# Causal mask added by VectorE instead of by a matmul, maximum subtracted by GpSimd, in a fused attention and mixture-of-experts kernel

## The reference, cut to what matters

```python
# x, ctx: (128, 64, 128); mask: (128, 64), all False here; 16 heads of 64
def xattn(q, k, v, Wq, Wk, Wv, Wo, bo, mask):       # q = layernorm(x), k = v = ctx
    dots = einsum('bhid,bhjd->bhij', qh, kh) * SCALE
    dots = where(mask[:, None, None, :], mask_value, dots)
    dots = where(causal[None, None, :, :], mask_value, dots)
    attn = softmax(dots, axis=-1)
    out = einsum('bhij,bhjd->bhid', attn, vh)
    return out.transpose(...).reshape(b, n, h * d) @ Wo + bo

x = x + xattn(layernorm(x), ctx, ctx, Wq, Wk, Wv, Wo, bo, mask)
x = x + moe(layernorm(x))        # router, top 2 of 8 experts, gelu, gate-weighted sum
```

## Time and profile before

| | us |
|---|---|
| median of 3 runs | 1299.99 |
| lowest and highest run | 1291.49, 1300.99 |
| profiled execution, its span from first to last instruction | 1169.6 |
| the 16 groups, within the span | about 35 to 870 |

### The profile page before, as it was taken

How to read it: one execution, slowest core, us unless ns; L and a number is a source line. 1 busy time by engine, 2 the same in 40 slices (tenths; PEclk the granted TensorE clock), 3 DMA queues, 4 the chain that set the end, 5 groups by cost and what they waited for, 6 DMA issues and landing times.

```text
span 1169.6 us, 24163 instructions
## 1 busy us (share of the span) xinstructions
PE 1052.8 (90%) x6755; PEld 718.1 (61%) x6755; DVE 786.0 (67%) x2372; ACT 706.3 (60%) x1373; POOL 496.6 (42%) x592
## 2 busy tenths in 40 slices
PE   7999999999999999999999999999955999999920
PEld 6655656565655656565665656566634888888820
DVE  4757595867768586866869586776755455545538
ACT  2676676767676676767667676767641544554410
POOL 3104344443424334442424344442253677776730
PEclk7899999999999999999999999999985999999965
DMA  6000101010010101001010101000012332223259
GB/s 187 19 19 1 38 1 36 7 29 25 11 36 0 36 0 36 11 25 36 0 36 0 36 5 32 16 20 19 1 55 83 85 91 88 87 87 88 77 171 282
DMA packets 80369, 55.93 MB, mean 48 GB/s; under 512 B 7620, under 2 KB 75606, under 8 KB 80342
## 3 DMA queue, kind: packets, MB, share of 16 engines
q1 hardware_dynamic: 70000, 37.01, 11.8%
q0 software_dynamic: 8704, 17.97, 4.4%
q10 hardware_dynamic: 1638, 0.62, 0.2%
HBM read 32.22 MB, written 23.35 MB: 48 GB/s over the span
## 4 chain that ended last, share of the span: by engine, by line
PE 67%; ACT 14%; issue 7%; DVE 6%; DMA 2%; POOL 1%; DVEq 1%; ACTq 0%; SPq 0%; POOLq 0%
PE bank L708 11%; PE bank L824 10%; PE bank L709 9%; PE bank L710 9%; ACT vf L634 7%; PE bank L958 6%; PE bank L810 6%; PE bank L961 5%; PE bank L799 4%; ACT pT L607 3%; ACT pr L612 3%; PE bank L821 3%; PE bank L938 2%; DVE xs L1337 2%; PE bank L736 1%
## 5 line engine op out<-in xcount | busy, mean ns | idle before, releaser
L634 ACT ACTIVATE vf<-bank 64x512 f32<-64x512 f32 x512 | 302.2, 590 | 91.2 <-PE bank L710 80.7
L461 POOL TENSOR_TENSOR rs<-ve,half 128x4 f32<-128x4 f32 x48 | 56.5, 1176 | 272.5 <-DVE ve L994 272.5
L620 ACT ACTIVATE kf<-bank 128x512 f32<-128x512 f32 x192 | 114.8, 598 | 94.3 <-PE bank L710 84.1
L550 POOL DMA_INDIRECT mixed<-kf,ix_i x144 | 142.7, 991 | 53.9 <-issue 50.2
L810 PE MATMUL bank<-vf,pT 128*64 128x128 f32 x2048 | 139.9, 279 | 8.3 <-ACT pT L607 6.0
L810 PEld LDWEIGHTS bank<-vf,pT 128*64 128x64 f32 x2048 | 109.7, 136 | 53.8 <-issue 33.6
L507 POOL DMA_INDIRECT slots<-zrow,slot_ix x120 | 122.5, 1021 | 42.4 <-issue 42.4
L824 PE MATMUL bank<-kf,zT 128*64 128x512 f32 x512 | 138.1, 618 | 0.0
L708 PE MATMUL bank<-cTh,Ah 128*128 128x512 f32 (+1 forms) x328 | 131.1, 400 | 5.4 <-DVE cTl L1060 5.4
L456 POOL TENSOR_TENSOR idle_p<-half 128x1 f32<-128x1 f32 x88 | 17.7, 202 | 247.9 <-DVE slot_ix L1167 224.3
L708 PE MATMUL bank<-Nh,cTh 128*128 128x512 f32 x256 | 120.6, 471 | 0.0
(11 more groups left out here) (187 smaller groups left out, 1912.5 us busy)
## 6 DMA issues: line engine op xcount, KB each, us to landing
kf<-slots SPq DMA_DIRECT2D x72, 130.0 KB
xs<-in_x_dram SPq DMA_DIRECT2D x16, 256.0 KB, 3.4
c_in<-in_ctx_dram SPq DMA_DIRECT2D x16, 256.0 KB, 3.8
kf<-mixed SPq DMA_DIRECT2D x16, 256.0 KB, 4.0
vf<-mixed SPq DMA_DIRECT2D x16, 256.0 KB, 4.1
out_dram<-xs SPq DMA_DIRECT2D x16, 256.0 KB, 3.6
mixed<-kf,ix_i POOLq DMA_INDIRECT x144
vf<-in_L_ffn_W_dram SPq DMA_DIRECT2D x2, 1024.0 KB, 9.6
```

What stands on the lines that cost most here:

```text
L550: pool.indirect_dma_start(out=mixed, out_offset=bass.IndirectOffsetOnAxis(ap=ix_i[buf][:, j:j + 1], axis=0), in_=y_sb[buf][:, j, :], in_of ...
L620: act.activation(kf[:, h, :], ring[gr.bank(name)][:, :], ACT.Copy).then_inc(act_ev, 1)
L634: act.activation(vf[par][64 * par_h:64 * par_h + 64, b, 4 * q4:4 * q4 + 4, :], ring[gr.bank(name)][64 * b:64 * b + 64, :].rearrange("p (j ...
```

## The change

- The mask matmul L821 and the bf16 identity `ident_b` (one memset and one select on POOL) go; the score matmuls start their banks themselves. PE waits for the new semaphore `masked` before it writes a score bank again, instead of for `shifted`.
- DVE's `shift_half` becomes `mask_half`: DVE adds `mask_b` to the scores on the way from PSUM to `pr` (SBUF), and takes the maximum from `pr`.
- A new function `shift` on POOL subtracts the maximum in place in `pr`, twice a pair, and releases ACT's exponential through `shifted`.
- The calls of `shift` are put between POOL's norms: pair 0 of a group after `x1_norm`, pair 1 after `z2_norm`, pairs 2 and 3 after `prep`, and `send` comes behind all four.
- Before its first group DVE waits for its own last write of `mask_b`.

```diff
@@ gpsimd
+            def shift(n, par):
+
+                for t in range(2):
+                    hs = slice(8 * t, 8 * t + 8)
+                    pool.wait_ge(sm_st, 6 * n + t + 1)
+                    pool.tensor_tensor(pr[par][:, hs, :], pr[par][:, hs, :],
+                                       mx[:, par, hs].unsqueeze(2).to_broadcast([P, 8, S]),
+                                       ALU.subtract).then_inc(shifted, 1)
...
             prep(0)
             prep(1, start.done("ZB"))
+            for i in range(GP):
+                shift(i, i % 2)
...
             with pool.Fori(2, NG - 1) as g:
                 x1_norm(g - 1)
+                shift(GP * g, 0)
                 z2_norm(g - 1)
+                shift(GP * g + 1, 1)
                 prep(g + 1, group_of(g - 1).done("ZB"))
+                shift(GP * g + 2, 0)
+                shift(GP * g + 3, 1)
                 next_tokens(g - 1)
                 send(g - 1)
@@ tensor, scores
-                    pe.wait_ge(shifted, 2 * n + hf - 1)
+                    pe.wait_ge(masked, 2 * n + hf - 1)
                 heads = s_ps[hf][:, :].rearrange("p (h s) -> p h s", s=S)
-                mrow = mask_b[:, n, :].unsqueeze(1).to_broadcast([P, 8, S])
-                pe.matmul(heads, ident_b[:, :], mrow, start=True, stop=False, skip_group_check=True)
                 for b in range(2):
                     cols = slice(i * P + 64 * b, i * P + 64 * b + 64)
                     last = pe.matmul(heads[64 * b:64 * b + 64], zT[:, cols], kf[:, 8 * hf:8 * hf + 8, cols],
-                                     start=False, stop=True, skip_group_check=True)
+                                     start=True, stop=True, skip_group_check=True)
@@ vector
-            def shift_half(n, par, t):
+            def mask_half(n, par, t):
...
                 dve.wait_ge(sc_ps, 2 * n + t + 1)
-                dve.reduce_max(mx[:, par, hs], src, AX_X).then_inc(sm_st, 1)
-                dve.wait_ge(sm_st, 6 * n + t + 1)
-                dve.tensor_tensor(pr[par][:, hs, :], src, mx[:, par, hs].unsqueeze(2).to_broadcast([P, 8, S]),
-                                  ALU.subtract).then_inc(shifted, 1)
+                dve.tensor_tensor(pr[par][:, hs, :], src, mask_b[:, n, :].unsqueeze(1).to_broadcast([P, 8, S]),
+                                  ALU.add).then_inc(masked, 1)
+                dve.wait_ge(masked, 2 * n + t + 1)
+                dve.reduce_max(mx[:, par, hs], pr[par][:, hs, :], AX_X).then_inc(sm_st, 1)
```

More of the change, by code:

```diff
@@ L122, in xattn_ffn_kernel @@
     out_t = out.rearrange("(n two) s d -> (two s) n d", two=2)
-    CONSTS = 10 + 2 * E + 3 + 7
+    CONSTS = 9 + 2 * E + 3 + 6
     TAB_NEXT, TAB_ALL = 1, 19
@@ L156, in xattn_ffn_kernel @@
         ident = sb("ident", [P, P])
-        ident_b = sb("ident_b", [P, P], BF16)
         causal = sb("causal", [P, P])
@@ L281, in xattn_ffn_kernel @@
         sm_st = sem("sm_st")
+        masked = sem("masked")
         shifted = sem("shifted")
@@ L416, in _ @@
             pool.memset(ident[:, :], 0.0).then_inc(consts, 1)
-            pool.memset(ident_b[:, :], 0.0).then_inc(consts, 1)
             pool.memset(causal[:, :], 0.0).then_inc(consts, 1)
@@ L435, in _ @@
                       allow_small_or_imprecise_dtypes=True).then_inc(consts, 1)
-            pool.wait_ge(consts, CONSTS - 7)
+            pool.wait_ge(consts, CONSTS - 6)
             pool.memset(pad_rows[:, :, D:D + 1], PAD_TOKEN).then_inc(consts, 1)
@@ L440, in _ @@
             pool.affine_select(out=ident[:, :], in_=ident[:, :], compare_op=ALU.not_equal, fill=1.0,
-                               base=0, pattern=[[-1, P]], channel_multiplier=1).then_inc(consts, 1)
-            pool.affine_select(out=ident_b[:, :], in_=ident_b[:, :], compare_op=ALU.not_equal, fill=1.0,
                                base=0, pattern=[[-1, P]], channel_multiplier=1).then_inc(consts, 1)
@@ L513, in _ @@
             prep(1, start.done("ZB"))
+            for i in range(GP):
+                shift(i, i % 2)
             x1_norm(0, first=True)
+            shift(GP, 0)
             z2_norm(0, first=True)
+            shift(GP + 1, 1)
             prep(2, group_of(0, True).done("ZB"))
+            shift(GP + 2, 0)
+            shift(GP + 3, 1)
             send(0)
@@ L524, in _ @@
             x1_norm(NG - 2)
+            shift(NP - 4, 0)
             z2_norm(NG - 2)
+            shift(NP - 3, 1)
+            shift(NP - 2, 0)
+            shift(NP - 1, 1)
             next_tokens(NG - 2)
@@ L1196, in group @@
                         dve.wait_ge(t_full, 2 * n - 2)
-                    shift_half(n, par, 0)
-                    shift_half(n, par, 1)
+                    mask_half(n, par, 0)
+                    mask_half(n, par, 1)
                     if i == 0:
@@ L1218, in _ @@
             dve.tensor_copy(next_slot[:, :], region[:, :]).then_inc(w1_ok, 1)
+            dve.wait_ge(mk_ok, 8)
             group(0, first=True)
```

## The result

| | median us | lowest to highest | runs |
|---|---|---|---|
| before, timed beside it | 1297.99 | 1291.49 to 1300.99 | 4 |
| after | 1321.72 | 1310.67 to 1326.12 | 4 |

A forecast was written before the change was run, and what follows sets the result against it. The pair phase was taken as a loop of latencies through four engines, with the exponential a station. 29 us in groups, 2 in the first group and 2 behind the last send made 33 us, so 1333 us, range 1318 to 1355.

The forecast's parts named there:

- The station on POOL: POOL's subtraction between DVE's maximum and ACT's exponential: 1.04 us each, exponential 2.64 us behind DVE's start, 1.19 us late.
- Pair 0, "no change to D1": D0 to D1, DVE's starts on pairs 0 and 1: taken as zero change, 0.7 us earlier to 0.9 later.
- Pair 1, +1.44: DVE's start on pair 1 to pair 2: 1.19 us exposed delay plus 0.25 for prep holding a DVE multiply.
- Pair 2, +0.20: DVE's start on pair 2 to pair 3: 0.52 us of delay shows, minus 0.32 for the mask matmul.
- Pair 3, +0.16: DVE's start on pair 3 to the next group's first head product: exponential at 2.64 us instead of 2.48.
- A group, +1.8: The four pairs' delays together, 1.8 us a group, 29 us for 16; the range was about 0.9 to 3 us.
- First group, 2 us: Pair 0's shift stands behind prep(1) on POOL, 2.6 us later than wanted, of which 2 us were taken.
- Behind the last send, 2 us (1 to 5): After the last group, x1_norm waits on POOL behind the later send, with no head phase to hide it: 2 us.
- With the 130.4 us around it: Time of the median outside the profiled span of 1169.6 us, added to the new span of about 1203 to give 1333.
- PE bounds: Rival, faster, 1267 us: PE's list limits the score matmuls, each removed one gives 0.23 to 0.32 us; chance 0.14.
- Within 1%: Rival, about 1305 us: gain and wait cancel through an early D1 and PE's returns, 0.5 us a group; chance 0.14.
- POOL is late: Rival, 1362 us: shifts of 1.27 us and multiplies of pairs 0 and 1 waiting for POOL, 3.9 a group; chance 0.12.

The follow-up runs named there:

- POOL's list reordered: The changed kernel with the addition to xs moved behind the shift of pair 1 and prep between the shifts of pairs 2 and 3: 1203.05 us, ratio 1.0278.
- the zeros: The changed kernel with one matmul of zeros with the mask put back before each score product, 128 in all: 1214.69 us, ratio 1.0363.
- after again: The changed kernel, unedited, run again on a chip of the experiments: 1224.27 us, ratio 1.0437 to the kernel before.
- PE kept busy behind the groups: The changed kernel plus 72 unused matmuls on PE between the last group and the expert stage: 1218.32 us, ratio 1.0385.
- before with `prep` later: The kernel before the change, with POOL's prep held until DVE has multiplied pair 2 of the group: 1167.13 us over 10 runs, ratio 0.9951.

## Why the prediction was right, and where its steps were off

The direction, the mechanism and the time (1333 forecast, 1321.72 measured) were right, the time partly by luck: the working gave 33 us, and the change costs 24 us in the timed runs of the result, near the lower end of the range (18), and 54 us, near its upper end, on the chip whose profiles look like the one that the working was read from. Within a group two errors nearly cancel: pair 0 came out 0.9 us lower than forecast and pair 1 1.07 higher. And nearly a third of what the profiled execution grew is the clock, for which the working had no term.

- **The station on POOL.** Right: 1043 ns at the median x128 where I took 1041, the exponential 2.57 us behind D0 where I had 2.64. By the factor two of the Trainium skill's GPSIMD Engine Reference (Engine selection) it would have been 1.38 us, an estimate; the measurement decides for one and a half.
- **Pair 0, "no change to D1".** Off: -0.9 us, just past the end of the range (-0.7). The step that failed is "they coincide with POOL's `z2_norm`": the second stretched multiply met `prep`, which the change moves away. `z2_norm` does run beside both multiplies now, but POOL pays: its L463 takes 1.55 us from 436.77, begun 0.04 us behind DVE's multiply. The port rule of SBUF — State Buffer in the Trainium skill (Who interferes with whom), that whoever issues first holds the port, fits both cases; I had used it for DVE's loss alone. It does not fit all: the multiply at 435.04 starts inside POOL's power of 128x4 (434.60, 1.01 us) and still takes 0.69. The working for a pair 0 without contention, D1 at D0 + 6.7, was good: it is 6.55.
- **Pair 1, +1.44.** The mechanism was right, the size not: +2.51. The station delays the exponential by 1.18 (1.19 forecast). Two terms failed. POOL's queue, put at nothing, is 0.64: `z2_norm`, moved behind two shifts, holds the shift of pair 1. Contention with `prep`, sized at 0.25, is about 0.6: the last multiply and the router instruction. The last 0.1 I cannot place. PE's wait of 1.17 us for `zrow` is new, but the run with POOL's list reordered has it too. I had written that POOL "is not free for the shift of pair 1 before D0 + 8.3" and used it only against an early D1. It came at D0 + 8.74, and D1 was early, so it counted.
- **Pair 2, +0.20.** Measured +0.35: the matmul gave 0.23, not 0.32, and the exposure is 0.58, not 0.52 (9.58 with the zeros against 9.00).
- **Pair 3, +0.16.** Measured +0.10. The head phase gave nothing back, as forecast (+0.12).
- **A group, +1.8.** Measured +2.18, inside 0.9 to 3. Those ends are not the sums of the terms as I gave them; added up, they make about 0.3 to 3.7.
- **First group, 2 us.** Measured 3.95: D1 - D0 there went from 6.13 to 9.10. POOL comes to the first shift at 51.97, behind `prep(1)`, and the 2.6 us of lateness pass in full. D2 - D1 adds 1.19, K0 - D3 0.25, and D3 - D2 gives 0.46 back.
- **Behind the last send, 2 us (1 to 5).** Measured 4.7, at the upper end. POOL in after again:

```profile
900.25 1.04 POOL L500 TENSOR_TENSOR pr<-pr,mx 128x512 f32<-128x512 f32 x1 [0.27 <-DVE mx L1093]
...
901.89 1.38 POOL L513 DMA_INDIRECT slots<-zrow,slot_ix  x1 [0.16 <-issue]
906.40 0.96 POOL L513 DMA_INDIRECT slots<-zrow,slot_ix  x1 [3.14 <-issue]
...
915.08 1.05 POOL L458 TENSOR_TENSOR rs<-ve,half 128x4 f32<-128x4 f32 x1
```

  The norm starts at 915.08, 17.64 us behind the last D3, against 12.98 before. The gap of 3.14 us behind the first scatter is in before again too (3.20). PE, which waited 10.24 us for its result before, waits 14.93.
- **What had no step: the clock.** About 7 us within groups and 10.6 at the start of the expert stage, nearly a third of the growth of the profiled execution. I had costed the removed matmul as time given back at most, and never asked what PE's emptier list does to the granted clock. Within groups the clock fell six times in after again, six times in after with PE kept busy behind the groups, and never with the zeros put back (the first group left out), so there the missing matmul has a part in it. It also never fell in before without any mask matmul, so the missing matmul alone does not bring it. At the start of the expert stage the loss is shown and its cause is not: it differs from execution to execution, and it went away in a kernel that has the same idle time there.
- **"With the 130.4 us around it".** Wrong, as said: 1.5 us lie around a span, and the profile was of an execution 130 us faster than the timed ones. The forecast stands without it, since it is 33 us on the median.
- **The rivals.** "PE bounds" is refuted by the matmul of zeros within after (0.23 us a group). In before it was half true: 15 us without the mask. "Within 1%" lacked the queue. "POOL is late" was too high in the groups (3.9, and 4.1 by its own terms), but its theme, POOL's list, is what cost half of what D2 - D1 grew.

**What stays open.** Why the change costs 24 us in one set of runs and 54 on the chip of after again. After's first profile differs from after again in three ways: each group is about 3.7 us longer, nearly all of it in the head phase (20.1 against 16.8); the clock falls at the end of nearly every group (0.58 from 488.66 to 490.66 in the group below); and it is lower in the expert stage:

```profile
1080.00:1100.00 20.00, 20.00 (x76) 16.64 (x76) 5.17 (x22) 5.15 (x14) 8.06 (x11) 0.50 0.17 52
```

In the head phase DVE and ACT stand still together, DVE here:

```profile
489.56 0.76 DVE L1078 TENSOR_TENSOR cTl<-bank,cTh 128x256 fp32r<-128x256 f32 x2 [2.39 <-ACT zT L591]
494.42 0.29 DVE L1083 TENSOR_TENSOR xs<-bank,xs 128x128 f32 x1 [4.10 <-remote]
```

while POOL runs its sends; what they wait for the profile does not name. There is no profile of before from that set of runs. If before has the same stall and the same low clock there, which its 1298 us suggest, then the change has less clock left to lose; that is argued, not shown.

## What to carry to other kernels

Work moved to an in-order engine costs three times: by its own duration on the path, by everything that is moved behind it on that engine, and by what the moved operations now run beside; lay the new list beside the old and ask of each operation who waits for it. Here a reordering of POOL's list brought the ratio from 1.0437 to 1.0278, a part of it by the clock, and moving one norm away from DVE's multiplies, with PE kept busy, beat the kernel before by 1.1%. A matmul that is off the path may still hold up the clock: before removing one, look at the granted clock in the stretches where PE is least busy. Take more than one execution's profile before you price the clock, since here one kernel's executions differ by 10 us with it. And compare an execution's span with its own time before adding anything to it.

## What the runs showed of the hardware

- At some group ends where PE had stood nearly idle (0.48 us busy of 2.00) the granted clock was near its lower level in the next 2 us (0.56), at others with the same idle time it was not (1.00). A kernel with 128 matmuls of zeros more took 10 us less (1224.27 and 1214.69, on two chips), and one with 72 unused ones behind the last group about 6 less (1218.32); most of the 10 us lie in a stretch where no matmul was added. The first 40 us or so of the expert stage had 0.65, 0.95, 0.91 and 1.00 in four kernels (after, with zeros, with unused matmuls, before) that compute the same there.
- Ten executions of one kernel on one chip (before with `prep` later) took 1161.75 to 1173.20 us, at mean granted clocks of 0.953 down to 0.942.
- Where a DVE operation with two SBUF inputs and a POOL operation of 128x512 overlapped, the one that started later was stretched: DVE 1.57 us instead of 0.69 beside `prep`, POOL 1.55 instead of 1.04 behind DVE's multiply, and 1.73 instead of 1.27. Beside POOL's 128x4 power, which had started first, DVE's multiply kept its 0.69 once.
- The same kernel took 1298 us in one set of runs and 1170 on three chips (medians 1169.81, 1170.94 and 1171.11).
